# First cross attention: where the seventh pair of row maxima stands, and in which PSUM set

## The chip, the cores and the metric

The kernel runs on one NeuronCore of a Trainium2 chip. The metric is the device time of one execution in microseconds; each figure without a profile is the median of several executions. The engines that matter here are TensorE (PE in the profile; PEld is its weight load), VectorE (DVE), ScalarE (ACT), GpSimd (POOL) and the DMA queues on SyncE (SP).

## What is computed

Four transformer layers in a row on x of 8 batches x 256 tokens x 256 channels. Only the cross attention of the first layer is touched. Cut to what matters:

```python
cq = heads(ci @ cq_w, NH, CHD)            # 8 batches, 16 heads of 8 channels, 256 queries
ck, cv = jnp.split(encoder_outputs @ ckv_w, 2, axis=-1)   # 1601 keys
scores = jnp.einsum('bhqd,bhkd->bhqk', q * scale, k)
p = jax.nn.softmax(scores, axis=-1)
cctx = jnp.einsum('bhqk,bhkd->bhqd', p, v)
```

## The kernel before

`cross_attention_0` does the work in 32 **units**: 8 batches times 4 groups (`NG`) of 4 heads. A unit n has these parts, all of them put on TensorE by hand in one order.

- **Keys.** Four chunks of 400 to 402 keys (`k_chunk`, L1336 to L1338, three matmuls each), split by ScalarE (`k_high`, L1140) and VectorE (L1242) into `ks`. The matmuls write half of PSUM set 1: `K_SET = (1, 1)`.
- **Maxima.** The softmax subtracts each query's maximum over all keys. The 16 items q0 to q15 (`maxima`) each make a pair of matmuls (L1357, two row groups of the array side by side) into a set of two banks, and VectorE takes both maxima in one reduction (L1254), which adds one to `maxed`. `M_SET[q]` names the set, `m_ps[0]` or `m_ps[1]`. Items 8 to 15 and 0 to 7 give two halves; `negative_maxima` closes each half (L1262).
- **Shift.** GpSimd spreads the maxima on a diagonal, `shift` (L1365) turns them on TensorE into set 1, VectorE adds them to the queries (L1269).
- **Scores and values.** 13 key tiles (`KT`). For each, `scores` makes two matmuls (L1377), ScalarE the exponentials (L1165), `values` (L1388) adds p times v in `av_ps`.
- **Sum.** After tile 12 VectorE copies the result (L1276). A matmul (L1503, into set 1, `SUM_SET`) picks the row sums, ScalarE takes the logarithm (L1172, `ln_ready`) and its exponential with a minus sign (L1178), GpSimd multiplies.

The units overlap. `step(u, nxt)` runs t = 1 to 13 over the tiles of unit u, and the place of every other item is in tables by t. `after` is the unit behind `nxt`:

- `max_at`: maxima of `nxt` (q7 at t = 1, q8 at t = 2, up to q14 and q15 at t = 8);
- `k_at`: key chunks of `after` at t = 2, 3, 5, 6;
- `max_after_at`: maxima of `after` already (q0 at t = 9 up to q6 at t = 13).

In a step TensorE has the scores of tile t + 1, the first item of `max_at`, the key chunk, the values of tile t, then what is left. Tile 13 and 14 of a unit are tiles 0 and 1 of the next. At t = 13 the order is: scores of the next unit's tile 1, values of its tile 0, the sum (L1503), and behind the sum q6 of `after`.

The text calls a **boundary** the stretch from the sum of one unit to the first key chunk, key (0,0), at t = 2 of the next step. An item waits until the one that used its set before was read. That is given by `FREED`, the number of reductions of that unit to be done. q7 waits at `FREED[7] = 7`, for the reduction of q6. key (0,0) waits for `ln_ready`: the sum in set 1 must be read.

Batches 0 to 5 run in a loop of three turns (`units`, two batches a turn), batches 6 and 7 are written out behind it. `ahead` starts unit 0 and the first maxima of unit 1.

Of the kernel before, what the change touches and what calls it, by code (L numbers as in the profile page):

```python
# [15 lines left out]
KT = -(-NK // P)  # L16
# [370 lines left out]
PRIME = 4  # L387
# [616 lines left out]
def cross_attention_0(nc, src, c, ph, early, ahead_, out_d):  # L1004
# [4 lines left out]
    with ph:  # L1009
# [11 lines left out]
        stored, ln_ready = ph.sems2("stored"), ph.sem("ln_ready")  # L1021
# [6 lines left out]
        NM = 4 * NC  # L1028
        ROWS = (slice(0, 64), slice(64, P))

        max_at = {1: (7,), 2: (8,), 3: (9,), 4: (10,), 5: (11,), 6: (12,), 7: (13,), 8: (14, 15)}
        max_after_at = {9: (0,), 10: (1, 2), 11: (3,), 12: (4, 5), 13: (6,)}
        M_SET = (0, 1, 0, 0, 1, 0, 0, 0, 0, 0, 0, 0, 0, 0, 0, 1)
        FREED = {2: 1, 3: 3, 5: 4, 6: 6, 7: 7, 8: 8, 9: 9, 10: 10, 11: 11, 12: 12, 13: 13, 14: 14}
        M_SET_AHEAD = tuple(q % 2 for q in range(NM))
        K_SET, K_SET_AHEAD, V_SET, SHIFT_SET, SUM_SET = (1, 1), (0, 1), (0, 1), 1, 1
        k_at, v_at, shift_at = {2: (0, 0), 3: (0, 1), 5: (1, 0), 6: (1, 1)}, 4, 11
# [14 lines left out]
        with nc.Block() as block:  # L1052
# [182 lines left out]
            def _(dve):  # L1235
# [63 lines left out]
                def ahead(u):  # L1299
                    second = following(u, NG)  # L1300
                    for i in range(2):
                        for h in range(2):
                            k_half(u, i, h, K_SET_AHEAD)
                    for q in range(NM):
                        maxima(u, q, M_SET_AHEAD)
                        if q == 8:
                            negative_maxima(u, 0)
                    negative_maxima(u, 1)
                    for i in range(2):
                        for h in range(2):  # L1310
                            k_half(second, i, h, K_SET_AHEAD)
                    maxima(second, 0, M_SET_AHEAD)
                    add_shift(u)
                    for q in range(1, 7):
                        maxima(second, q, M_SET_AHEAD)

                def step(u, nxt):
# [6 lines left out]
            def _(pe):  # L1324
# [67 lines left out]
                def max_item(nxt, after, q):  # L1392

                    n = nxt[3]
                    if q == 11 and nxt[2] == 0:
                        pe.wait_ge(cv_ready, nxt[0] * 2 + 1 + PRIME)
                    elif q == 15 and after:
                        pe.wait_ge(k_ready, after[3] * 4 + 4 + PRIME)
                    elif q == 15:
                        pe.wait_ge(ln_ready, n - 1 + PRIME)  # L1400
                    else:
                        pe.wait_ge(maxed, n * NM + FREED[q] + PRIME)
                    maxima(nxt, q)
# [10 lines left out]

                def key_item(nxt, after, i, h):
                    if i == 0 and h == 0:
                        pe.wait_ge(ln_ready, nxt[3] - 1 + PRIME)
                    elif i == 1 and nxt[2] == 0 and h == 0:
                        pe.wait_ge(cv_ready, nxt[0] * 2 + 2 + PRIME)
                    elif i == 1 and nxt[2]:  # L1420
                        pe.wait_ge(k_ready, after[3] * 4 + h + 1 + PRIME)
                    k_chunk(after, i, h)
# [11 lines left out]
                def ahead(u):  # L1434
# [16 lines left out]
                    pe.wait_ge(cv_ready, 2 + PRIME)  # L1451
                    scores(tile(u, None, 0))
                    scores(tile(u, None, 1))
                    for q in range(1, 7):
                        if q == 1:
                            pe.wait_ge(shifted, 1 + PRIME)
                        else:
# [5 lines left out]
                def step(u, nxt):  # L1463
                    b, p, g, n = u
                    after = nxt and following(nxt, NG)
                    for t in range(1, KT + 1):
# [21 lines left out]
                        if nxt and nxt[2] == 0 and t == v_at:  # L1488
# [1 line left out]
                            values_made(nxt, 0)  # L1490
                            pe.wait_ge(k_ready, after[3] * 4 + 2 + PRIME)
                            values_made(nxt, 1)
                        for q in later[first:] if t < KT else ():
                            max_after_item(nxt, after, q)
                    pe.wait_ge(av_copied, n + 1 + PRIME)

# [4 lines left out]
                    else:  # L1501
                        pe.wait_ge(ln_ready, n + PRIME)
                    nc.tensor.matmul(m_ps[SUM_SET][:, 0:S], c["sum8"][:], av[:], start=True, stop=True).then_inc(sum_ready, 1)  # L1503
                    if after:
                        for q in max_after_at[KT]:
                            max_after_item(nxt, after, q)

                units(pe, NG, ahead, step)

# [1819 lines left out]
```

## Time and profile before

| what | us |
|---|---|
| median of 3 executions | 3669.23 |
| lowest and highest | 3666.94, 3672.79 |
| the profiled execution, its own time | 3663.52 |
| its span, first to last instruction | 3661.7 |
| TensorE busy, all stages | 3410.2 (93%) |
| VectorE busy | 2020.0 (55%) |
| ScalarE busy | 1840.7 (50%) |
| first cross attention | about 430 to 1255 us of the span |

The page gives busy time for the whole program, which has many stages. For one stage one reads the timeline of each engine in the same window and compares starts. A group "x2" is two instructions merged into one row. Matmuls overlap, so the distance from one start to the next is what a piece costs, and not its duration.

### The profile page before, as it was taken

Reading aid. Unit: us, or ns where it says so; the run is one execution under the profiler, and the core shown is the slowest. Engines: PE = TensorE matmul, PEld = TensorE weight load, DVE = VectorE, ACT = ScalarE, POOL = GpSimd, SP = SyncE. Lnnn points to the kernel's source line nnn. Section 1 sums busy time; section 2 is a strip of 40 time slices with the busy share of each in tenths; the row PEclk is TensorE's granted clock in tenths of the full one; section 3 lists DMA queues with packets and bytes.
Section 4 is the critical chain, followed back from the end, with each engine's and each line's share of the span. In section 5 each row is a group of like instructions: output and inputs, shape, how many; then the busy total and the mean of one; then the engine's idle time right before and its main releaser. Section 6 shows DMA issues by size and latency. Waiting matters only on the chain. (4 is left out here: it accounts for less than half of the span.)

```text
span 3661.7 us, 74076 instructions
## 1 busy us (share of the span) xinstructions
PE 3410.2 (93%) x25048; PEld 2314.4 (63%) x25048; DVE 2020.0 (55%) x3324; ACT 1840.7 (50%) x3374; POOL 1588.5 (43%) x1421
## 2 busy tenths in 40 slices
PE   7798889898999799989999999999999998999997
PEld 5555644444444388866666666666666665878886
DVE  4455577677777454435555555555555553113454
ACT  2244367666677534335555555555555553333333
POOL 3212112122211011116777777777777775004554
PEclk9899899999999899989999999999999999999998
DMA  4775200000000212230000000000001002210200
GB/s 122 166 111 116 100 7 16 18 17 18 18 16 27 96 74 99 101 117 7 16 31 13 32 13 31 13 32 13 31 14 59 13 13 103 88 68 16 97 7 12
DMA packets 74751, 179.36 MB, mean 49 GB/s; under 512 B 14720, under 2 KB 44928, under 8 KB 68480
## 3 DMA queue, kind: packets, MB, share of 16 engines
q1 hardware_dynamic: 70240, 161.81, 14.6%
q0 software_dynamic: 4128, 12.60, 1.3%
q8 instruction: 221, 3.62, 0.4%
q14 instruction: 162, 1.33, 0.1%
HBM read 115.09 MB, written 59.26 MB: 48 GB/s over the span
## 5 line engine op out<-in xcount | busy, mean ns | idle before, releaser
L1652 POOL TENSOR_TENSOR cross_acc<-cross_acc,cross_probs 128x512 f32<-128x512 f32 (+1 forms) x704 | 920.6, 1308 | 160.3 <-ACT cross_probs L1715 118.9
L1715 ACT ACTIVATE cross_probs<-cross_s,cross_bias 128x512 f32<-128x512 f32 (+1 forms) x832 | 529.6, 684 | 490.0 <-PE cross_s L1934 488.2
L1811 DVE TENSOR_REDUCE cross_partmax<-cross_r 128x1 f32<-128x400 f32 (+1 forms) x1024 | 541.8, 570 | 343.1 <-PE cross_r L1904 325.2
L1254 DVE TENSOR_REDUCE cross_partmax<-cross_m 128x2 f32<-128x800 f32 (+1 forms) x512 | 497.1, 992 | 186.4 <-PE cross_m L1357 185.4
L1165 ACT ACTIVATE cross_probs<-cross_s 128x512 f32<-128x512 f32 (+1 forms) x832 | 453.5, 595 | 151.2 <-PE cross_s L1377 150.9
L1947 PE MATMUL cross_av<-cross_probs,cross_v 128*64 128x256 f32 (+1 forms) x3328 | 458.1, 393 | 0.0
L1947 PEld LDWEIGHTS cross_av<-cross_probs,cross_v 128*64 128x64 f32 (+1 forms) x3328 | 199.2, 136 | 172.7 <-ACT cross_probs L1715 76.6
L1104 POOL TENSOR_TENSOR cross_diag<-c_ident,cross_negmax 128x256 fp32r<-128x256 f32 x128 | 75.8, 613 | 495.0 <-DVE cross_negmax L1262 495.0
L1388 PE MATMUL cross_av<-cross_probs,cross_v 128*32 128x256 f32 (+1 forms) x3328 | 268.9, 395 | 10.0 <-ACT cross_probs L1165 8.5
L1928 PE MATMUL cross_s<-cross_q_hi,cross_k_hi 64*128 64x256 f32 (+1 forms) x1664 | 253.5, 299 | 0.0
L1800 DVE TENSOR_TENSOR cross_k_lo<-cross_r,cross_k_hi 128x400 fp32r<-128x400 f32 (+1 forms) x256 | 146.5, 572 | 192.1 <-ACT cross_k_hi L1693 192.1
L1357 PE MATMUL cross_m<-cross_ks,cross_qd 64*128 64x400 f32 (+1 forms) x1024 | 211.1, 417 | 43.2 <-DVE cross_partmax L1254 35.1
L1934 PE MATMUL cross_s<-cross_shf,c_ones_r 64*128 64x256 f32 (+1 forms) x1664 | 236.5, 278 | 0.0
L1932 PE MATMUL cross_s<-cross_q_hi,cross_k_lo 64*128 64x256 f32 (+1 forms) x1664 | 236.2, 278 | 0.0
L1930 PE MATMUL cross_s<-cross_q_lo,cross_k_hi 64*128 64x256 f32 (+1 forms) x1664 | 236.0, 278 | 0.0
L1904 PE MATMUL cross_r<-cross_k_hi,cross_q_hi 64*128 64x400 f32 (+1 forms) x1024 | 212.9, 399 | 5.4 <-issue 5.3
L1377 PE MATMUL cross_s<-cross_qd,cross_ks 64*128 64x512 f32 (+1 forms) x832 | 202.8, 472 | 9.1 <-issue 8.6
L1928 PEld LDWEIGHTS cross_s<-cross_q_hi,cross_k_hi 64*128 64x128 f32 (+1 forms) x1664 | 155.0, 181 | 75.1 <-issue 71.6
L1357 PEld LDWEIGHTS cross_m<-cross_ks,cross_qd 64*128 64x128 f32 x1024 | 97.4, 190 | 153.9 <-DVE cross_partmax L1254 114.8
L2356 PE MATMUL tail_in<-tail_xe,tail_wi 128*128 128x256 f32 x768 | 173.3, 381 | 3.5 <-DVE tail_xe L2260 3.5
L1904 PEld LDWEIGHTS cross_r<-cross_k_hi,cross_q_hi 64*128 64x128 f32 x1024 | 101.5, 186 | 111.1 <-issue 83.1
L2356 PEld LDWEIGHTS tail_in<-tail_xe,tail_wi 128*128 128x128 f32 x768 | 146.9, 191 | 24.5 <-DVE tail_xe L2260 4.2
(307 smaller groups left out, 6504.2 us busy)
## 6 DMA issues: line engine op xcount, KB each, us to landing
d_masked_ctx<-tail_ctx_split SPq DMA_DIRECT2D x8, 1602.0 KB, 5.3
d_self_qk<-selfproj_qk_split POOLq DMA_DIRECT2D x32, 256.0 KB, 5.5
self_qs<-d_self_qk SPq DMA_DIRECT2D x64, 128.0 KB, 7.7
self_ks<-d_self_qk SPq DMA_DIRECT2D x64, 128.0 KB, 8.3
d_cross<-tail_pr SPq DMA_DIRECT2D x8, 1024.0 KB, 4.6
cross_qp<-d_cross SPq DMA_DIRECT2D x64, 128.0 KB, 2.2
d_cross<-cross_out SPq DMA_DIRECT2D x64, 128.0 KB, 1.8
tail_attn<-d_cross SPq DMA_DIRECT2D x8, 1024.0 KB, 5.4
```

The lines of the kernel that those rows point to most:

```text
L1165: nc.scalar.activation(probs[0:w, buf, 2 * r:2 * r + 2], s_ps[bank(of_tile, r)][0:w].rearrange("p (h s) -> p h s", h=2), ACT.Exp, scale=CH ...
L1254: nc.vector.tensor_reduce(partmax[:, :, jt // 2, jt % 2, i:i + 1], m_pair(sets[q], w), AX.X, ALU.max).then_inc(maxed, 1)
L1357: last = nc.tensor.matmul(m_ps[sets[q]][:, r * 512:r * 512 + w], qd[ROWS[r], g, j, t * P:(t + 1) * P], ks[ROWS[r], g, k0:k0 + w], start=Tr ...
L1388: last = nc.tensor.matmul(av_ps[32 * j:32 * j + 32, 0:S], v[0:w, p, t, 4 * g + j], probs[0:w, (g * KT + t) % 4, j], start=(t == 0), stop=( ...
L1652: nc.gpsimd.tensor_tensor(acc[0:w, g % 2], left, probs[0:w, slot % NPB], ALU.add).then_inc(added, 1)
L1715: nc.scalar.activation(probs[0:w, (g * KT + t) % NPB], src_, ACT.Exp, scale=XHD ** -0.5, bias=bias[0:w, p, t:t + 1]).then_inc(probs_ready, 1)
L1811: nc.vector.tensor_reduce(partmax[:, m, i:i + 1], r_ps[MAX_BANK[q]][:, 0:KCH[i][1]], AX.X, ALU.max).then_inc(maxed, 1)
L1904: nc.tensor.matmul(r_ps[MAX_BANK[q]][:, 0:w], q_hi[ROWS[h], g % 2, t * P:(t + 1) * P], k_hi[ROWS[h], g % 2, k0:k0 + w], start=True, stop=T ...
L1928: nc.tensor.matmul(o[h], k_hi[ROWS[h], x, keys], q_hi[ROWS[h], x], start=True, stop=False)
L1934: last = nc.tensor.matmul(o[h], c["ones_r"][ROWS[h], 0:w], shf[ROWS[h], x], start=False, stop=True)
L1947: last = nc.tensor.matmul(av_ps[h * XHD:(h + 1) * XHD, 0:S], v[0:w, g // 4, t, d0:d0 + XHD], probs[0:w, (g * KT + t) % NPB, h], start=(t = ...
L2356: last = nc.tensor.matmul(in_ps[n % 3][:, h * S:(h + 1) * S], wi[2 * e + h][:, k, t * P:(t + 1) * P], xe[:, b % 2, e, k], start=(k == 0), ...
```

## The change

q6 of the unit behind, which stood behind the sum at t = 13, goes to the first step of the next unit (t = 1): behind the scores of tile 2 and ahead of the values of tile 1. q7 goes behind those values, and from set 0 to set 1. The waits follow:

- q7 waits for `ln_ready` (the sum in set 1 was read) in place of the reduction of q6;
- q8 waits for seven reductions, that of q6, since q6 used set 0 before it;
- key (0,0) waits for eight reductions, that of q7, in place of `ln_ready`.

`ahead` makes q1 to q5 of unit 1 in place of q1 to q6. No matmul, reduction or activation is added or taken away. The diff:

```diff
--- before.py
+++ after.py
@@ -1028,10 +1028,10 @@
         NM = 4 * NC
         ROWS = (slice(0, 64), slice(64, P))
 
-        max_at = {1: (7,), 2: (8,), 3: (9,), 4: (10,), 5: (11,), 6: (12,), 7: (13,), 8: (14, 15)}
-        max_after_at = {9: (0,), 10: (1, 2), 11: (3,), 12: (4, 5), 13: (6,)}
-        M_SET = (0, 1, 0, 0, 1, 0, 0, 0, 0, 0, 0, 0, 0, 0, 0, 1)
-        FREED = {2: 1, 3: 3, 5: 4, 6: 6, 7: 7, 8: 8, 9: 9, 10: 10, 11: 11, 12: 12, 13: 13, 14: 14}
+        max_at = {1: (6, 7), 2: (8,), 3: (9,), 4: (10,), 5: (11,), 6: (12,), 7: (13,), 8: (14, 15)}
+        max_after_at = {9: (0,), 10: (1, 2), 11: (3,), 12: (4, 5)}
+        M_SET = (0, 1, 0, 0, 1, 0, 0, 1, 0, 0, 0, 0, 0, 0, 0, 1)
+        FREED = {2: 1, 3: 3, 5: 4, 6: 6, 7: 5, 8: 7, 9: 9, 10: 10, 11: 11, 12: 12, 13: 13, 14: 14}
         M_SET_AHEAD = tuple(q % 2 for q in range(NM))
         K_SET, K_SET_AHEAD, V_SET, SHIFT_SET, SUM_SET = (1, 1), (0, 1), (0, 1), 1, 1
         k_at, v_at, shift_at = {2: (0, 0), 3: (0, 1), 5: (1, 0), 6: (1, 1)}, 4, 11
@@ -1311,7 +1311,7 @@
                             k_half(second, i, h, K_SET_AHEAD)
                     maxima(second, 0, M_SET_AHEAD)
                     add_shift(u)
-                    for q in range(1, 7):
+                    for q in range(1, 6):
                         maxima(second, q, M_SET_AHEAD)
 
                 def step(u, nxt):
@@ -1392,7 +1392,9 @@
                 def max_item(nxt, after, q):
 
                     n = nxt[3]
-                    if q == 11 and nxt[2] == 0:
+                    if q == 7:
+                        pe.wait_ge(ln_ready, nxt[3] - 1 + PRIME)
+                    elif q == 11 and nxt[2] == 0:
                         pe.wait_ge(cv_ready, nxt[0] * 2 + 1 + PRIME)
                     elif q == 15 and after:
                         pe.wait_ge(k_ready, after[3] * 4 + 4 + PRIME)
@@ -1414,7 +1416,7 @@
 
                 def key_item(nxt, after, i, h):
                     if i == 0 and h == 0:
-                        pe.wait_ge(ln_ready, nxt[3] - 1 + PRIME)
+                        pe.wait_ge(maxed, nxt[3] * NM + 8 + PRIME)
                     elif i == 1 and nxt[2] == 0 and h == 0:
                         pe.wait_ge(cv_ready, nxt[0] * 2 + 2 + PRIME)
                     elif i == 1 and nxt[2]:
@@ -1451,7 +1453,7 @@
                     pe.wait_ge(cv_ready, 2 + PRIME)
                     scores(tile(u, None, 0))
                     scores(tile(u, None, 1))
-                    for q in range(1, 7):
+                    for q in range(1, 6):
                         if q == 1:
                             pe.wait_ge(shifted, 1 + PRIME)
                         else:
@@ -1490,7 +1492,7 @@
                             values_made(nxt, 0)
                             pe.wait_ge(k_ready, after[3] * 4 + 2 + PRIME)
                             values_made(nxt, 1)
-                        for q in later[first:] if t < KT else ():
+                        for q in later[first:]:
                             max_after_item(nxt, after, q)
                     pe.wait_ge(av_copied, n + 1 + PRIME)
 
@@ -1501,9 +1503,6 @@
                     else:
                         pe.wait_ge(ln_ready, n + PRIME)
                     nc.tensor.matmul(m_ps[SUM_SET][:, 0:S], c["sum8"][:], av[:], start=True, stop=True).then_inc(sum_ready, 1)
-                    if after:
-                        for q in max_after_at[KT]:
-                            max_after_item(nxt, after, q)
 
                 units(pe, NG, ahead, step)
```

On TensorE, at a boundary inside the loop (m0 and m1 are the two sets, s0 to s2 the banks of the scores, av0 that of the values; rows of semaphore registers are left out). Before:

```order
1363 L1503 MATMUL cross0_m1<-cross0_av,c_sum8 128x256
...
1365 L1357 MATMUL cross0_m0<-cross0_ks,cross0_qd 128x400 x2
...
1367 L1377 MATMUL cross0_s1<-cross0_qd,cross0_ks 128x512
...
1369 L1377 MATMUL cross0_s2<-cross0_qd,cross0_ks 128x512
...
1371 L1357 MATMUL cross0_m0<-cross0_ks,cross0_qd 128x402 x2
...
1373 L1388 MATMUL cross0_av0<-cross0_probs,cross0_v 32x256 x4
...
1379 L1357 MATMUL cross0_m0<-cross0_ks,cross0_qd 128x400 x2
1380 L1336 MATMUL cross0_m1<-cross0_c_hi,cross0_wk_hi 128x400
```

After:

```order
1364 L1505 MATMUL cross0_m1<-cross0_av,c_sum8 128x256
...
1366 L1377 MATMUL cross0_s1<-cross0_qd,cross0_ks 128x512
...
1368 L1377 MATMUL cross0_s2<-cross0_qd,cross0_ks 128x512
...
1370 L1357 MATMUL cross0_m0<-cross0_ks,cross0_qd 128x400 x2
...
1372 L1388 MATMUL cross0_av0<-cross0_probs,cross0_v 32x256 x4
1373 L1357 MATMUL cross0_m1<-cross0_ks,cross0_qd 128x402 x2
...
1379 L1357 MATMUL cross0_m0<-cross0_ks,cross0_qd 128x400 x2
1380 L1419 REGISTER_ALU
1381 L1336 MATMUL cross0_m1<-cross0_c_hi,cross0_wk_hi 128x400
```

The pair of 400 columns (q6) went behind both scores, the pair of 402 (q7) behind the values and into m1, and the key chunk has a wait of its own (L1419).

On VectorE, the reductions behind the copy L1276 keep their number and order. Those of q6, q7, q8 before:

```order
444 L1254 TENSOR_REDUCE cross0_partmax<-cross0_m0 128x2
445 L1251 REGISTER_ALU
446 L1254 TENSOR_REDUCE cross0_partmax<-cross0_m0 128x2
447 L1251 REGISTER_ALU
448 L1253 REGISTER_ALU
449 L1254 TENSOR_REDUCE cross0_partmax<-cross0_m0 128x2
450 L1262 TENSOR_REDUCE cross0_negmax<-cross0_partmax 128x4
```

After:

```order
445 L1254 TENSOR_REDUCE cross0_partmax<-cross0_m0 128x2
446 L1251 REGISTER_ALU
447 L1254 TENSOR_REDUCE cross0_partmax<-cross0_m1 128x2
448 L1251 REGISTER_ALU
449 L1253 REGISTER_ALU
450 L1254 TENSOR_REDUCE cross0_partmax<-cross0_m0 128x2
451 L1262 TENSOR_REDUCE cross0_negmax<-cross0_partmax 128x4
```

Only the set that the middle one reads is another.

## Rows read from the trace of the kernel before

**Rows 1.** The page, busy time: engine, us, share of the span, instructions.
```profile
PE 3410.2 (93%) x25048; PEld 2314.4 (63%) x25048; DVE 2020.0 (55%) x3324; ACT 1840.7 (50%) x3374; POOL 1588.5 (43%) x1421
```

**Rows 2.** Busy time by stretch: us, each engine's busy us, clock, DMA share, GB/s.
```profile
490.00:665.00 175.00, 160.43 (x1322) 74.02 (x1314) 134.08 (x170) 122.34 (x231) 36.41 (x51) 1.00 0.05 13
671.00:700.00 29.00, 27.23 (x199) 12.10 (x203) 21.06 (x27) 18.38 (x35) 6.29 (x9) 0.85 0.11 36
```

**Rows 3.** Line 1503, the sum: matmul passes, ns least/median/most, first and last start in us.
```profile
L1503 PE MATMUL cross_m<-cross_av,c_sum x64: 379/416/483, 490.4 to 1252.5; 128*128 128x256 f32 x64
```

**Rows 4.** Timeline of TensorE at one boundary: start, us, engine, line, tiles, count, [idle before].
```profile
817.61 0.70 PE L1503 MATMUL cross_m<-cross_av,c_sum 128*128 128x256 f32 x2 [0.17 <-DVE cross_partmax L1254]
818.51 0.45 PE L1357 MATMUL cross_m<-cross_ks,cross_qd 64*128 64x400 f32 x2 [0.20 <-DVE cross_partmax L1254]
818.80 0.41 PE L1377 MATMUL cross_s<-cross_qd,cross_ks 64*128 64x512 f32 x2
820.05 0.46 PE L1357 MATMUL cross_m<-cross_ks,cross_qd 64*128 64x402 f32 x2 [0.85 <-DVE cross_partmax L1254]
820.44 0.64 PE L1388 MATMUL cross_av<-cross_probs,cross_v 128*32 128x256 f32 x8
821.01 0.50 PE L1377 MATMUL cross_s<-cross_qd,cross_ks 64*128 64x512 f32 x2
821.60 0.45 PE L1357 MATMUL cross_m<-cross_ks,cross_qd 64*128 64x400 f32 x2
821.97 0.45 PE L1336 MATMUL cross_m<-cross_c_hi,cross_wk_hi 128*128 128x400 f32 x1
```

**Rows 5.** The same boundary, VectorE.
```profile
816.57 1.88 DVE L1254 TENSOR_REDUCE cross_partmax<-cross_m 128x2 f32<-128x800 f32 x2
819.00 0.99 DVE L1254 TENSOR_REDUCE cross_partmax<-cross_m 128x2 f32<-128x800 f32 x1 [0.55 <-PE cross_m L1357]
820.55 1.00 DVE L1254 TENSOR_REDUCE cross_partmax<-cross_m 128x2 f32<-128x804 f32 x1 [0.55 <-PE cross_m L1357]
822.17 0.99 DVE L1254 TENSOR_REDUCE cross_partmax<-cross_m 128x2 f32<-128x800 f32 x1 [0.63 <-PE cross_m L1357]
...
824.01 0.99 DVE L1254 TENSOR_REDUCE cross_partmax<-cross_m 128x2 f32<-128x800 f32 x1 [0.77 <-PE cross_m L1357]
```

**Rows 6.** The same boundary, ScalarE.
```profile
818.35 0.38 ACT L1172 ACTIVATE cross_ln_sum<-cross_m 128x256 f32<-128x256 f32 x1 [0.76 <-PE cross_m L1503]
818.63 0.59 ACT L1165 ACTIVATE cross_probs<-cross_s 128x512 f32<-128x512 f32 x1
819.10 0.42 ACT L1178 ACTIVATE cross_rsum<-cross_ln_sum 128x256 f32<-128x256 f32 x1
819.41 1.08 ACT L1165 ACTIVATE cross_probs<-cross_s 128x512 f32<-128x512 f32 x2
```

**Rows 7.** Waits of 430 to 1260 us: total, times, longest.
```profile
PEld cross_m L1357 <- DVE cross_partmax L1254: 114.8, 228, 1.3
```

**Rows 8.** Timeline of TensorE after the sum of the 31st unit.
```profile
1236.90 0.70 PE L1503 MATMUL cross_m<-cross_av,c_sum 128*128 128x256 f32 x2
1237.53 0.50 PE L1377 MATMUL cross_s<-cross_qd,cross_ks 64*128 64x512 f32 x2
1238.56 0.64 PE L1388 MATMUL cross_av<-cross_probs,cross_v 128*32 128x256 f32 x8 [0.53 <-ACT cross_probs L1165]
```

**Rows 9.** Timeline of TensorE at a boundary outside the loop.
```profile
1140.61 0.67 PE L1503 MATMUL cross_m<-cross_av,c_sum 128*128 128x256 f32 x2
...
1144.88 0.45 PE L1336 MATMUL cross_m<-cross_c_hi,cross_wk_hi 128*128 128x400 f32 x1
```

**Rows 10.** Timeline of TensorE where the loop turns.
```profile
665.38 0.45 PE L1357 MATMUL cross_m<-cross_ks,cross_qd 64*128 64x400 f32 x2 [0.20 <-DVE cross_partmax L1254]
669.73 0.91 PE L1377 MATMUL cross_s<-cross_qd,cross_ks 64*128 64x512 f32 x2 [3.90 <-issue]
...
672.96 0.70 PE L1336 MATMUL cross_m<-cross_c_hi,cross_wk_hi 128*128 128x400 f32 x1
```

## The prediction, made before the changed kernel ran

> **What bounds the kernel now.** I read the page first, then the stage. TensorE is busy 93% of the whole span [rows 1]. In 175 us of the first cross attention it is busy 160.43 us and VectorE 134.08 us [rows 2]: TensorE sets the pace, VectorE has slack, and the question is where TensorE stands still. The list of waits has one place above TensorE's others: weight loads of the maxima that wait for a VectorE reduction, 114.8 us in 228 times [rows 7]. Loads run ahead of matmuls, so that total is partly covered. The timeline shows what is not.
>
> At a boundary inside the loop [rows 4] times run from the start of the sum, 817.61, taken as 0: q6 at 0.90, scores of tile 2 at 1.19, q7 at 2.44, values of tile 1 at 2.83, scores of tile 3 at 3.40, q8 at 3.99, key (0,0) at 4.36. TensorE was idle 0.20 us before q6 and 0.85 before q7, and between scores of tile 3 and q8 lie 0.59 us, though a pair of scores lasts 0.50. All three are one chain through PSUM set 0 [rows 5]: q6's reduction starts at 819.00 and lasts 0.99, q7 starts 0.06 behind its end; q7's starts at 820.55 and lasts 1.00, q8 follows 0.05 behind its end. A turn of the chain is 1.54 us (820.05 less 818.51), of which TensorE can fill only the scores. VectorE itself waits for TensorE in each turn (0.55, 0.55, 0.63 us). So neither engine is full: the handshake over one set is the bound. There are 32 sums (64 passes, two each, 490.4 to 1252.3 us) [rows 3], and 30 of them have a q6 behind them.
>
> **The change, part by part.** I go through the new order with the rows' own distances.
>
> *Scores of tile 2 go first behind the sum.* In the 31st unit no q6 follows, and there the scores start 0.63 behind the sum (1237.53 less 1236.90) [rows 8]. Their banks are free. New: 0.63 in place of 1.19.
>
> *q6 behind these scores.* The scores last 0.50, so q6 stands at 1.13 at the latest. Its wait, q5's reduction, is over at 818.45 (816.57 + 1.88), or 0.84 [rows 5]. Its issue takes 0.29 (818.80 less 818.51), so TensorE is free at 1.42. It costs nothing, since the next piece is late anyway:
>
> *Values of tile 1* need the exponentials of tile 1. The second of them stands behind the logarithm of the sum, starts at 818.63 and lasts 0.59, to 1.61 [rows 6]. In the 31st unit, where nothing else holds them, the values start at 1.66 (1238.56 less 1236.90), after 0.53 us idle, released by ScalarE [rows 8]. New: 1.66 in place of 2.83. The cover of q6 is this wait; were it gone, q6 would cost its 0.29.
>
> *q7 behind the values, in set 1.* Values to the next piece is 0.57 (821.01 less 820.44) [rows 4], so q7 starts at 2.23. Its new wait, the logarithm, ends at 818.73, or 1.12 [rows 6]: free. Queued behind this wait on TensorE is everything, and it costs nothing as long as the logarithm is over 1.1 us early. q7's reduction starts 0.50 behind q7 (820.55 less 820.05), at 2.73; q6's was over by 1.13 + 0.49 + 0.99 = 2.61. It ends at 3.73.
>
> *Scores of tile 3, then q8.* Scores at 2.23 + 0.29 = 2.52. Exponentials of tile 2 run from 819.41, the first over by 2.34 [rows 6], so their banks are free too. q8 follows within 0.59, at 3.11 at the latest, with its wait (q6's reduction, 2.61) over, and takes 0.37 to the next piece: TensorE is free at 3.48.
>
> *key (0,0) has a new wait*, for q7's reduction: 3.73 + 0.06 = 3.79. It is met 0.3 us after TensorE is free, so it now ends the boundary. Behind it wait on TensorE the values of tile 2, and then ScalarE's and VectorE's halves of the key. New: 3.79 in place of 4.36, a gain of 0.57 us. No row shows this wait, so it has bounds. Above: values at 1.61, the end of the exponential itself, gain 0.62. Below: the 0.09 us by which the loop's boundary is longer than the one outside [rows 4, 9] once more, and 0.1 for a semaphore that comes late, gain 0.38. I take 0.57, since each link has a row of its own kind. That it could be a loss is a rival below.
>
> *Outside the loop* the same boundary takes 4.27 (1144.88 less 1140.61) [rows 9], and the new chain the same 3.79: gain 0.48.
>
> *Does the gain last?* From key (0,0) on nothing is moved. VectorE's next reduction (q9, 824.01) waited 0.77 us for TensorE [rows 5], so it shifts with it; q8's reduction, chained behind q7's, now ends near 4.65, and q9 is made later than that. No engine has a start of its own that would hold TensorE back.
>
> *Where the loop turns* (two times) TensorE waits for instructions: 3.90 us idle [rows 10]. From 669.73 (scores of tile 2) to 672.96 (key) are 3.23 us, at a lower clock: the stretch of 671 to 700 us has 0.85 [rows 2]. Now the break begins before q6, about 0.6 us earlier, but q6 (0.58 there) and the reduction of q7 (some 0.7 us) lie behind it. I put it at 0, between a gain and a loss of 0.5 each.
>
> *The start*: one maximum fewer in front, one more in step 0. 0.3 us by the same chain, between 0 and 0.6. *The last such boundary* has no key; there q9 waits for q8's reduction, and I take 0.7.
>
> **The sum.** 24 loop units less the two turns are 22 boundaries: 22 x 0.57 = 12.5. Outside, 5 x 0.48 = 2.4. Last 0.7, start 0.3, turns 0. Together 15.9 us. The profiled execution took 3663.52 and would take 3647.6; the median shown is 5.7 us above it, and 3669.2 - 15.9 gives 3653.
>
> **A rule that speaks against it.** The traced stretch with seven such boundaries, each with stops of 0.20 and 0.85 us, shows a granted clock of 1.00, that is 2.4 GHz [rows 2]. The changed boundary has stops of about 0.24 and 0.3 us. The Trainium skill, "TensorE: Matmul & The Clock Gate", section "A second HAM failure mode: psum-queue depth-cycling", says that an engine which idles briefly again and again, cycling through PSUM, can swing between its two levels. By that rule TensorE could run some of these units at 1.2 GHz; the trace of before disagrees for longer stops of the same kind.
>
> **The rivals.**
> *Eaten later (neutral).* The 0.57 us come back as a wait for ScalarE or VectorE within the next steps. For: ScalarE's exponentials release the values in the 31st unit [rows 8] and may do so in other steps. Against: VectorE's idle time is released by TensorE [rows 5], and between ScalarE's exponentials of tile 2, over by 2.9, and the key lie 0.9 us. 3664 to 3672.
> *Partly.* Slips of 0.2 to 0.4 us: a late q7, register instructions that outlast their cover, the turns. Gain 5 to 11 us: 3658 to 3664.
> *Slower: the key is held by the late q7.* The new order ties key (0,0) to ScalarE: exponential of tile 1, values, q7, reduction, key. If the values start later than 1.66 + 0.57 = 2.23, the boundary is longer than before; each 0.1 us beyond costs 3 us in 30 boundaries. At 2.6 it is 11 us: 3680. For: the ScalarE part sits behind the sum, its logarithm and a copy on VectorE. Against: 1.66 in the 31st unit, and 1.61 from ScalarE's own rows [rows 6, 8]: two readings that agree.
> *Slower: the clock swings.* TensorE falls to 1.2 GHz at the boundaries. Behind the turn, at a lower clock, scores of tile 2 to the key take 3.23 us with no wait [rows 10]; at the full clock they take 3.17, of which 0.85 is q7's wait [rows 4]. So such a boundary has 0.9 us more of TensorE's own work, and 30 of them 27, against 15.9 gained: 3680. It decides when some 18 boundaries are hit. For it speaks only the 0.85 behind the turn [rows 2], which follows a break of 3.90 us, ten times the new stops. The rule named above is the one that would give this rival.
>
> **How the numbers follow.** Forecast as summed, gain 11 to 19 us: 0.68. Partly: 0.15. Eaten: 0.09. Late q7: 0.04. Clock: 0.02. More than 19 us: 0.02. The bound of what can be told from no change is 0.2%, 7.3 us: faster than 3661.9. Of "partly" four fifths lie beyond it. Faster 0.82, same 0.12, slower 0.06. The range takes the forecast with the spread of the medians (3666.9 to 3672.8, three either side) and most of "partly": 3647 to 3661.
>
> **What would show it.** In the changed profile: scores of tile 2 at 0.6 behind the sum, values of tile 1 at 1.66, q7 at 2.23, key at 3.8, released by a VectorE reduction; some 746 us from the first to the last sum in place of 762 [rows 3]; the same distances behind the key as before. Values later than 1.8, or a key more than 0.1 behind q7's reduction, would show a step wrong; a new stop on TensorE between t = 3 and 12 would show "eaten".

## The result and the profile after

| | median us | lowest, highest | executions |
|---|---|---|---|
| before | 3668.39 | 3666.94, 3672.79 | 4 |
| after | 3638.35 | 3634.26, 3649.83 | 4 |

The first measurement gave a ratio of 0.9921, 95% interval 0.9897 to 0.9945: 30 us faster, where 16 were forecast, and under the low end of the range. The profiled execution took 3649.83 us, span 3648.1, that is 13.7 us less than the profiled one of before. Two further measurements of the same kernel, 12 executions each on two other occasions (chips 7 and 1), gave 0.9965 (0.9949 to 0.9980) and 0.9952 (0.9936 to 0.9969), medians 3644.16 and 3641.94, some 13 and 18 us faster. Every figure here leaves out one slow execution, of the kernel with the order alone (5671.55 us at a mean granted clock of 0.751). So there are two questions: is the mechanism the forecast one, and where did the first 30 us come from?

The page of the kernel after, busy time (answers to [rows 1]), and TensorE's row for the sum, now line 1505: ns least, median, most, then first and last start (answers to [rows 3]):

```profile
PE 3398.7 (93%) x25048; PEld 2313.2 (63%) x25048; DVE 2016.5 (55%) x3324; ACT 1843.3 (51%) x3374; POOL 1590.2 (44%) x1421
...
L1505 PE MATMUL cross_m<-cross_av,c_sum x64: 379/416/483, 498.8 to 1243.6; 128*128 128x256 f32 x64
```

From the first to the last pass are 744.8 us, against 762.1 before: 17.3 less, where the forecast had some 746 in place of 762. That this near hit has compensating parts in it is shown further down. The weight loads of the maxima wait less for VectorE (answer to [rows 7]):

```profile
PEld cross_m L1357 <- DVE cross_partmax L1254: 53.0, 142, 1.9
```

Timeline of TensorE at one boundary inside the loop, the kernel after (answers to [rows 4]; start, us, engine, line, operation, count, idle before and its releaser):

```profile
793.96 0.70 PE L1505 MATMUL cross_m<-cross_av,c_sum 128*128 128x256 f32 x2
794.59 0.50 PE L1377 MATMUL cross_s<-cross_qd,cross_ks 64*128 64x512 f32 x2
794.93 0.38 PE L1357 MATMUL cross_m<-cross_ks,cross_qd 64*128 64x400 f32 x2
795.62 0.64 PE L1388 MATMUL cross_av<-cross_probs,cross_v 128*32 128x256 f32 x8 [0.32 <-ACT cross_probs L1165]
796.19 0.45 PE L1357 MATMUL cross_m<-cross_ks,cross_qd 64*128 64x402 f32 x2
796.48 0.43 PE L1377 MATMUL cross_s<-cross_qd,cross_ks 64*128 64x512 f32 x2
796.71 0.38 PE L1357 MATMUL cross_m<-cross_ks,cross_qd 64*128 64x400 f32 x2
797.74 0.45 PE L1336 MATMUL cross_m<-cross_c_hi,cross_wk_hi 128*128 128x400 f32 x1 [0.65 <-DVE cross_partmax L1254]
```

Read from the sum as 0: scores of tile 2 at 0.63, q6 at 0.97, values of tile 1 at 1.66, released by ScalarE, q7 at 2.23, scores of tile 3 at 2.52, q8 at 2.75, key (0,0) at 3.78, released by VectorE. Forecast: 0.63, 1.13 at the latest, 1.66, 2.23, 2.52, 3.11 at the latest, 3.79.

VectorE at the same place (answers to [rows 5]):

```profile
795.35 0.99 DVE L1254 TENSOR_REDUCE cross_partmax<-cross_m 128x2 f32<-128x800 f32 x1 [0.55 <-PE cross_m L1357]
796.68 1.89 DVE L1254 TENSOR_REDUCE cross_partmax<-cross_m 128x2 f32<-128x804 f32 x2 [0.34 <-PE cross_m L1357]
798.49 0.16 DVE L1262 TENSOR_REDUCE cross_negmax<-cross_partmax 128x4 f32<-128x16 f32 x1
799.77 0.99 DVE L1254 TENSOR_REDUCE cross_partmax<-cross_m 128x2 f32<-128x800 f32 x1 [1.12 <-PE cross_m L1357]
```

The reductions of q7 and q8 are now one row of two, back to back. Before, each of them stood 0.55 to 0.63 us behind a wait of its own. The next one (q9) waits 1.12 us for TensorE, so VectorE does not hold the steps behind.

At 9 of the 22 boundaries inside the loop the key stands 0.09 to 0.11 us later, at 3.86 to 3.88. One of them, where the sum starts at 521.96, VectorE and then the key:

```profile
524.68 1.89 DVE L1254 TENSOR_REDUCE cross_partmax<-cross_m 128x2 f32<-128x804 f32 x2 [0.35 <-PE cross_m L1357]
...
525.82 0.44 PE L1336 MATMUL cross_m<-cross_c_hi,cross_wk_hi 128*128 128x400 f32 x1 [0.73 <-DVE cross_partmax L1254]
```

q7's reduction starts 2.72 behind the sum as at the other boundaries and lasts 0.99 to 1.00, but the key follows 0.14 behind its end in place of 0.06. That is the prediction's sign of a wrong step, "a key more than 0.1 behind q7's reduction". Why it happens at the same places of each turn was not found out.

ScalarE (answers to [rows 6]) is where it was, 0.74, 1.02 and 1.49 behind the sum:

```profile
794.70 0.38 ACT L1172 ACTIVATE cross_ln_sum<-cross_m 128x256 f32<-128x256 f32 x1 [0.76 <-PE cross_m L1505]
794.98 0.59 ACT L1165 ACTIVATE cross_probs<-cross_s 128x512 f32<-128x512 f32 x1
795.45 0.42 ACT L1178 ACTIVATE cross_rsum<-cross_ln_sum 128x256 f32<-128x256 f32 x1
```

What the stage does not explain lies ahead of it. The first sum stands at 498.8 us in this execution, against 490.4 before, although no instruction ahead of the stage was changed. The stretch of 10 to 430 us, before and then after (us, busy us of each engine, clock, DMA share, GB/s), holds the same 2248 matmuls:

```profile
10.00:430.00 420.00, 348.93 (x2248) 249.26 (x2248) 218.53 (x414) 141.01 (x278) 92.93 (x98) 0.92 0.58 127
```
```profile
10.00:430.00 420.00, 353.75 (x2248) 251.44 (x2248) 218.02 (x413) 139.46 (x276) 93.05 (x98) 0.91 0.57 125
```

The same matmuls took 4.8 us more of TensorE at a lower granted clock. The kernel before, run again, has its first sum at 500.3 us, so this belongs to the execution and not to the change. A single execution can lose or win as much as half of what this change is worth.

### The profile page after: what moved, and what is told of

It is laid out like the page before. It is cut to its first block and busy times, and to the rows that moved or that the text cites. A ratio compares the mean times of both kernels' runs of the same rounds, so it can differ in the third digit from the quotient of the medians.

```text
span 3648.1 us, 74076 instructions
## 1 busy us (share of the span) xinstructions
PE 3398.7 (93%) x25048; PEld 2313.2 (63%) x25048; DVE 2016.5 (55%) x3324; ACT 1843.3 (51%) x3374; POOL 1590.2 (44%) x1421
## 3 DMA queue, kind: packets, MB, share of 16 engines
q8 instruction: 221, 3.62, 0.4%
```

## The experiments

Twelve runs on three chips (7, 13 and 1), each against 19 to 29 executions of the kernel before on its own chip. "Mean clock" is TensorE's granted clock, the mean over a run's executions (of the profiled one alone in the two rows of first profiles). "Key" is the start of key (0,0) behind the sum at a boundary inside the loop, "stage" the time from the first to the last sum of the profiled execution, in us. The stage is read from one execution, to the first pass of the last sum; the last pass, used above, starts 0.4 later.

| kernel | key | stage | ratio to before | 95% interval | mean clock |
|---|---|---|---|---|---|
| before (first profile) | 4.36 | 761.7 | | | 0.968 |
| after (first profile) | 3.78 | 744.5 | | | 0.967 |
| before again | 4.36 | 758.6 | 1.0007 | 0.9993, 1.0021 | 0.970 |
| after again | 3.77 | 741.9 | 0.9965 | 0.9949, 0.9980 | 0.970 |
| after, third time | 3.77 | 744.7 | 0.9952 | 0.9936, 0.9969 | 0.971 |
| new order alone | 4.36 | 773.8 | 1.0038 | 1.0019, 1.0056 | 0.966 |
| new order alone, again | 4.36 | 772.6 | 1.0028 | 1.0009, 1.0046 | 0.966 |
| new set alone | 3.33 | 731.9 | 0.9934 | 0.9914, 0.9954 | 0.970 |
| after, ScalarE 0.3 later | 4.08 | 753.6 | 0.9986 | 0.9966, 1.0006 | 0.968 |
| before, ScalarE 0.3 later | 4.36 | 757.2 | 1.0012 | 0.9997, 1.0028 | 0.970 |
| after, exponential first | 3.39 | 732.3 | 0.9917 | 0.9885, 0.9950 | 0.971 |
| new set, exponential first | 3.34 | 731.4 | 0.9933 | 0.9908, 0.9958 | 0.969 |
| new set, key behind values | 3.63 | 724.9 | 0.9921 | 0.9891, 0.9951 | 0.968 |
| the same again | 3.62 | 724.7 | 0.9917 | 0.9897, 0.9937 | 0.969 |

### Each kernel once more

No edit. What was expected of the kernel before:

> The kernel before once more, nothing changed. It tells how far two profiles and two medians of the same kernel lie apart. Theory A (the first cross attention gained 17 us, what lies beyond it in the medians is TensorE's low-clock stretches falling elsewhere in other stages): ratio to the kernel before 1.000 within 0.2%, but single executions and the stages outside differ by up to 10 us with the mean clock. Theory B (the change moves other stages too): the executions agree within 3 us and the stages outside the first cross attention take the same time in each profile of this kernel.

Measured: ratio 1.0007, and single executions from 3651.45 us (clock 0.973) to 3673.74 (clock 0.968). The first cross attention took 758.6 against 761.7 in the first profile. Theory A holds in that executions of one kernel differ by 20 us. The median of these 12, 3664.37, is 7 us above that of the 29 others of the same kernel on the same chip, 3657.26.

> The changed kernel once more. Theory A: from the first to the last sum again 744.5 us within 1.5, and the median 14 to 20 us under the kernel before, since the 30 us of the first measurement were 17 from the change and the rest from clock stretches of those executions. Theory B: again some 30 us under, with stages outside the first cross attention shorter by a fixed amount of 10 us or more.

Measured: 0.9965 and a stage of 741.9 us, 16.7 under the kernel before run again. The median of 3644.16 is 13 us under that of before. Both are just outside what theory A named (14 to 20 us, and a stage of 744.5 within 1.5), and far from theory B's 30.

> The changed kernel a third time. Theory A (the change is worth what the stage shows, 16 to 17 us; the first medians differed by more since few executions were compared and each one's mean clock moves it by up to 15 us): first to last sum 742 to 745 us, ratio to before 0.9955, 0.994 to 0.998. Theory B (something else is gained outside the stage): ratio at or under 0.993.

Measured: 0.9952, stage 744.7. Theory A. In both repeats the interval excludes the 0.993 of theory B, and the first measurement's 0.9921 as well.

The executions show what separates them. The 89 of the kernel before that stand in these runs reach from 3643.15 us at a mean granted clock of 0.976 (chip 7) to 3679.78 at 0.966 (chip 13). The 41 on chip 7 alone reach from 3643.15 to 3673.74. A line through all 192 executions of all kernels, one slope and a level for each kernel, has 2.6 us for 0.001 of mean clock and leaves 3.1 us unexplained. The text calls the difference between two levels of this line the difference **at equal clock**. For the changed kernel it is 15.8 us under before, give or take 1.5. Two things limit it. It is a relation over these runs, not an experiment with a single cause changed. And where a kernel itself brings more low clock, as the next one does, this figure leaves that loss out.

The first four executions of the changed kernel fit this. Three of them ran at a mean clock of 0.973 or 0.974, where the 24 later ones have 0.9706 on average. The later ones at 0.973 or 0.974 took 3633.58 to 3644.85 us, and the three took 3634.26 to 3638.67.

### The order alone

The changed kernel with q7 back in set 0 and the waits of before:

```diff
-        M_SET = (0, 1, 0, 0, 1, 0, 0, 1, 0, 0, 0, 0, 0, 0, 0, 1)
-        FREED = {2: 1, 3: 3, 5: 4, 6: 6, 7: 5, 8: 7, 9: 9, 10: 10, 11: 11, 12: 12, 13: 13, 14: 14}
+        M_SET = (0, 1, 0, 0, 1, 0, 0, 0, 0, 0, 0, 0, 0, 0, 0, 1)
+        FREED = {2: 1, 3: 3, 5: 4, 6: 6, 7: 7, 8: 8, 9: 9, 10: 10, 11: 11, 12: 12, 13: 13, 14: 14}
...
-                    if q == 7:
-                        pe.wait_ge(ln_ready, nxt[3] - 1 + PRIME)
-                    elif q == 11 and nxt[2] == 0:
+                    if q == 11 and nxt[2] == 0:
...
-                        pe.wait_ge(maxed, nxt[3] * NM + 8 + PRIME)
+                        pe.wait_ge(ln_ready, nxt[3] - 1 + PRIME)
```

> The changed kernel with the seventh pair back in set 0: q7 waits for q6's reduction, q8 for q7's, key (0,0) for the logarithm, as before; only the order on TensorE is the new one. Theory (the set is what gains): q7 at 2.50, q7's reduction over at 4.0, q8 at 4.05, key at 4.42 behind the sum against 4.36 before: no gain, 0 to 3 us slower than before. Rival (the order gains, by putting work beside the wait): key near 3.8, 15 us faster.

Timeline of TensorE at a boundary of this kernel:

```profile
809.08 0.70 PE L1503 MATMUL cross_m<-cross_av,c_sum 128*128 128x256 f32 x2 [0.17 <-DVE cross_partmax L1254]
809.70 0.50 PE L1377 MATMUL cross_s<-cross_qd,cross_ks 64*128 64x512 f32 x2
810.05 0.38 PE L1357 MATMUL cross_m<-cross_ks,cross_qd 64*128 64x400 f32 x2
810.74 0.64 PE L1388 MATMUL cross_av<-cross_probs,cross_v 128*32 128x256 f32 x8 [0.31 <-ACT cross_probs L1165]
811.52 0.45 PE L1357 MATMUL cross_m<-cross_ks,cross_qd 64*128 64x402 f32 x2
811.81 0.40 PE L1377 MATMUL cross_s<-cross_qd,cross_ks 64*128 64x512 f32 x2
813.07 0.45 PE L1357 MATMUL cross_m<-cross_ks,cross_qd 64*128 64x400 f32 x2 [0.85 <-DVE cross_partmax L1254]
813.44 0.45 PE L1336 MATMUL cross_m<-cross_c_hi,cross_wk_hi 128*128 128x400 f32 x1
```

The wait of 0.85 us did not go. It moved from q7 to q8, and the key stands at 4.36 (813.44 less 809.08) as before, where 4.42 was expected. The order by itself gains nothing: the set gains. What was not expected (0 to 3 us) is that it is 0.28% to 0.38% slower, 10 to 14 us, with the same key. So it ran once more:

> The new order with q7 in set 0 once more. The first time its key stood at 4.36 as before and yet it was 0.38% slower, at a lower mean clock (0.966 against 0.970). Theory (its longer stops bring TensorE to its lower level more often): mean clock again under 0.968 and the time 5 to 15 us over before. Rival (chance of the executions): clock 0.970 and the time within 4 us of before.

Measured again: 1.0028, mean clock 0.966. The theory holds against chance. At equal clock the two runs are 1.5 us over before, give or take 1.6: nearly all of the loss goes with the lower clock. The stage in both profiled executions has a lower clock than before, here the kernel before and then the two of the order alone, over the stage:

```profile
430.00:1255.00 825.00, 745.85 (x5968) 343.31 (x5968) 606.78 (x768) 556.76 (x1050) 150.67 (x216) 0.97 0.06 17
```
```profile
430.00:1280.00 850.00, 756.28 (x5972) 350.37 (x5971) 608.34 (x770) 559.64 (x1051) 150.65 (x216) 0.95 0.06 17
```
```profile
430.00:1280.00 850.00, 755.90 (x5972) 350.22 (x5972) 607.66 (x769) 559.52 (x1051) 150.77 (x216) 0.95 0.06 17
```

TensorE's busy time grew by 10 us for the same matmuls. One of the falls, behind a boundary:

```profile
736.42 0.45 PE L1357 MATMUL cross_m<-cross_ks,cross_qd 64*128 64x400 f32 x2 [0.86 <-DVE cross_partmax L1254]
736.80 0.53 PE L1336 MATMUL cross_m<-cross_c_hi,cross_wk_hi 128*128 128x400 f32 x1
...
737.92 1.08 PE L1388 MATMUL cross_av<-cross_probs,cross_v 128*32 128x256 f32 x8
```

The values take 1.08 us in place of 0.64. Here the prediction's clock rival is seen at work, in a kernel whose stops at a boundary are 0.31, some 0.2 and 0.85 us, a little more than the 0.20 and 0.85 of before. At the plain boundaries of the changed kernel, whose stops are 0.32 and 0.65, none of its three profiles has such a fall. Behind the rows: the Trainium skill, "TensorE: Matmul & The Clock Gate", section "A second HAM failure mode: psum-queue depth-cycling", says that an engine with many brief stops can swing between its levels. These rows agree for the order alone and not for the plain boundaries of the changed kernel. What exactly decides stays open.

Two places of the changed kernel do lose by the clock. The first is the start of the stage, 32 us from the first scores, before and then after:

```profile
458.00:490.00 32.00, 27.90 (x199) 12.57 (x200) 23.22 (x30) 17.58 (x33) 2.37 (x4) 0.79 0.00 1
```
```profile
465.00:497.00 32.00, 27.74 (x186) 12.54 (x186) 22.03 (x28) 16.71 (x31) 2.37 (x4) 0.74 0.00 1
```

In the same time it gets 186 matmuls done and not 199. From the first scores to the first sum are 31.4 and 31.6 us in the two profiles of before, 31.3 with the set alone, 32.8 to 32.9 in the three of the changed kernel, and 33.3 and 33.4 in the two of the order alone: the new order costs 1.3 us there or more. The second place is the second turn of the loop, 28 us of before and then of after:

```profile
864.00:892.00 28.00, 23.59 (x184) 10.35 (x184) 19.40 (x25) 17.43 (x33) 3.09 (x5) 0.94 0.12 39
```
```profile
860.00:888.00 28.00, 23.87 (x168) 10.74 (x166) 17.08 (x22) 15.96 (x30) 3.10 (x5) 0.82 0.12 39
```

The third profile of the changed kernel has 0.82 here too, the second 0.94 as before. The other way round, the kernel before falls once at a plain boundary outside the loop, in both of its profiles, and the changed one in none:

```profile
1193.00:1205.00 12.00, 11.32 (x77) 5.16 (x77) 7.24 (x10) 7.78 (x15) 1.91 (x3) 0.86 0.06 15
```

### The set alone

The kernel before with q7 in set 1 and its waits, q6 left behind the sum:

```diff
-        M_SET = (0, 1, 0, 0, 1, 0, 0, 0, 0, 0, 0, 0, 0, 0, 0, 1)
-        FREED = {2: 1, 3: 3, 5: 4, 6: 6, 7: 7, 8: 8, 9: 9, 10: 10, 11: 11, 12: 12, 13: 13, 14: 14}
+        M_SET = (0, 1, 0, 0, 1, 0, 0, 1, 0, 0, 0, 0, 0, 0, 0, 1)
+        FREED = {2: 1, 3: 3, 5: 4, 6: 6, 7: 5, 8: 7, 9: 9, 10: 10, 11: 11, 12: 12, 13: 13, 14: 14}
...
-                    if q == 11 and nxt[2] == 0:
+                    if q == 7:
+                        pe.wait_ge(ln_ready, nxt[3] - 1 + PRIME)
+                    elif q == 11 and nxt[2] == 0:
...
-                        pe.wait_ge(ln_ready, nxt[3] - 1 + PRIME)
+                        pe.wait_ge(maxed, nxt[3] * NM + 8 + PRIME)
...
-                            pe.wait_ge(maxed, NM + q - 1 + PRIME)
+                            pe.wait_ge(maxed, NM + q - 1 + (q == 6) + PRIME)
```

> The kernel before with the seventh pair in set 1 and its three waits, q6 left behind the sum as before (the sixth pair of the start waits for the fifth's reduction). Theory (the set is what gains, and the new order costs, since it puts q7 behind values that wait for ScalarE): q6 at 0.90, q7 at 1.5, its reduction over at 3.3, key at 3.4 against 4.36 before and 3.77 after: 22 x 0.96 + 5 x 0.9 = 26 us under before, 9 to 11 under the changed kernel. Rival (both parts are needed): key at 3.8 or later, no better than the changed kernel.

```profile
787.33 0.70 PE L1505 MATMUL cross_m<-cross_av,c_sum 128*128 128x256 f32 x2 [0.16 <-DVE cross_partmax L1254]
788.22 0.45 PE L1357 MATMUL cross_m<-cross_ks,cross_qd 64*128 64x400 f32 x2 [0.20 <-DVE cross_partmax L1254]
788.51 0.42 PE L1377 MATMUL cross_s<-cross_qd,cross_ks 64*128 64x512 f32 x2
788.74 0.37 PE L1357 MATMUL cross_m<-cross_ks,cross_qd 64*128 64x402 f32 x2
789.04 0.64 PE L1388 MATMUL cross_av<-cross_probs,cross_v 128*32 128x256 f32 x8
...
790.66 0.45 PE L1336 MATMUL cross_m<-cross_c_hi,cross_wk_hi 128*128 128x400 f32 x1 [0.21 <-DVE cross_partmax L1254]
```

The key is at 3.33 (790.66 less 787.33), the stage 731.9 us, 30 under the first profile of before and 12.6 under after. The ratio of 0.9934 is 24 us under before. At equal clock it is 26, and 10 under after (give or take 3). The ratios' intervals just touch, 0.9914 to 0.9954 and 0.9949 to 0.9980 on this chip, but key and stage say the same. So half of the change, the other set, is worth more than the whole. The new order costs some 10 us of it, since it puts q7 behind values that wait for ScalarE; the exponential first, below, takes this wait away, and the stage is then as short as here.

### ScalarE later

One more ScalarE instruction behind each unit's logarithm, first in the kernel after, then in that of before (`spare` is a buffer that nobody reads, `spare_ready` its semaphore):

```diff
                     nc.scalar.activation(ln_sum[:], m_ps[SUM_SET][:, 0:S], ACT.Ln).then_inc(ln_ready, 1)
+                    act.wait_ge(spare_ready, n + PRIME)
+                    nc.scalar.activation(spare[:].rearrange("p (t s) -> p t s", t=2),
+                        c["ident"][:].unsqueeze(1).to_broadcast([P, 2, P]), ACT.Copy).then_inc(spare_ready, 1)
```

> The changed kernel with one more ScalarE instruction behind the logarithm of each unit, a copy of a constant 128x256 into a buffer that nobody reads. It puts the second exponential of tile 1 later by its own start-to-start time, some 0.28 us. Theory (key (0,0) hangs on the chain exponential, values, q7, reduction): values of tile 1 at 1.94 behind the sum, q7 at 2.51, key at 4.05; 30 boundaries x 0.28 = 8 us slower than the changed kernel, so 7 us under before. Rival (VectorE or TensorE has another reason for 3.77): key stays at 3.8 and the time with it.

The kernel after with it, values of tile 1 and then the key:

```profile
795.52 0.70 PE L1508 MATMUL cross_m<-cross_av,c_sum 128*128 128x256 f32 x2 [0.17 <-DVE cross_partmax L1257]
...
797.48 0.64 PE L1391 MATMUL cross_av<-cross_probs,cross_v 128*32 128x256 f32 x8 [0.62 <-ACT cross_probs L1166]
...
799.60 0.45 PE L1339 MATMUL cross_m<-cross_c_hi,cross_wk_hi 128*128 128x400 f32 x1 [0.65 <-DVE cross_partmax L1257]
```

The values went from 1.66 to 1.96, the key from 3.78 to 4.08: every 0.1 us of ScalarE arrives at the key in full. In the time it is 9 us at equal clock (expected 8). That is the price law of the rival "key held by the late q7".

> The kernel before with the same spare ScalarE instruction behind the logarithm, 0.28 us in each unit. Theory: before the change the boundary hung on the chain through set 0, and the values of tile 1 stood behind q7 at 2.82 with the exponential long over: key stays at 4.36, time within 2 us of before. Rival (the instruction itself costs, wherever it stands, so that the 9 us of the changed kernel with it prove nothing): 6 us or more slower.

In the kernel before the key stayed at 4.36 and the stage at 757.2 us. The ratio of 1.0012 (0.9997 to 1.0028) is 4 us and allows from none to 10, so by itself it does not rule out the rival, 6 us or more. At equal clock it is 2.5 us, give or take 1.9, against 9 in the changed kernel, and that does. The stage agrees: it is the shortest of the three profiles with a key at 4.36 and both pairs in the order of before. The instruction costs where the chain goes through ScalarE, and not for itself.

### The exponential first

ScalarE makes the second exponential of tile 1 ahead of the logarithm:

```diff
-                    if before and t == 1:
-                        log_sum(before)
...
                     if now:
                         exponentials(now, 1)
                     if before and t == 1:
+                        log_sum(before)
                         inverse_sum(before)
```

> The changed kernel with ScalarE's logarithm moved behind the second exponential of tile 1, which no longer waits for the sum. Theory: values of tile 1 follow q6 on TensorE at 1.3 to 1.4, q7 at 1.9, its reduction chained to q6's from 2.4 to 3.4, key at 3.45 against 3.77: 29 x 0.32 = 9 us under the changed kernel. Rival: the logarithm now comes later or another wait takes over, key at 3.77 or later.

```profile
788.49 0.70 PE L1504 MATMUL cross_m<-cross_av,c_sum 128*128 128x256 f32 x2 [0.17 <-DVE cross_partmax L1253]
...
789.76 0.64 PE L1387 MATMUL cross_av<-cross_probs,cross_v 128*32 128x256 f32 x8
...
791.88 0.45 PE L1335 MATMUL cross_m<-cross_c_hi,cross_wk_hi 128*128 128x400 f32 x1 [0.51 <-DVE cross_partmax L1253]
```

Measured on top of the changed kernel: values of tile 1 at 1.27, with no wait, q7 at 1.84, key at 3.39, stage 732.3, ratio 0.9917. At equal clock 13 us under after, where 9 were expected; the stage is 10 to 12 us shorter. The theory holds.

> Both: the seventh pair in set 1 with the order of before, and the logarithm behind the exponential. Theory: there q7 stands ahead of the values, and the key hangs on the two chained reductions of q6 and q7, not on ScalarE: key at 3.35 as without the second edit, time within 2 us of the seventh pair in set 1 alone. Rival (ScalarE holds TensorE there too): 5 us or more faster than that.

On top of the set alone: key at 3.34 and stage 731.4 against 3.33 and 731.9; ratio 0.9933 against 0.9934. The theory holds there too: with q7 ahead of the values ScalarE is off the path, and what is left is the pair of reductions of q6 and q7.

### The key behind the values

On top of the set alone, key (0,0) behind the values of tile 2:

```diff
-                        if after and t in k_at:
+                        if after and t in k_at and t > 2:
                             key_item(nxt, after, *k_at[t])
...
                         if now:
                             values(now)
+                        if after and t == 2:
+                            key_item(nxt, after, *k_at[t])
```

> The seventh pair in set 1 with the order of before, and key (0,0) behind the values of tile 2 in place of ahead of them, so that the values fill the wait for q7's reduction. Theory: values of tile 2 at 3.0 (released by ScalarE at 2.94), key at 3.55 with no wait, scores of tile 4 at 4.3 against 4.65: 29 x 0.35 = 10 us under the seventh pair in set 1 alone, some 35 under before. Rival: the later key makes ScalarE's and VectorE's halves late, and a new stop at t = 3 to 5 takes it back.

```profile
780.77 0.70 PE L1507 MATMUL cross_m<-cross_av,c_sum 128*128 128x256 f32 x2
...
783.83 0.64 PE L1388 MATMUL cross_av<-cross_probs,cross_v 128*32 128x256 f32 x8
784.40 0.45 PE L1336 MATMUL cross_m<-cross_c_hi,cross_wk_hi 128*128 128x400 f32 x1
```

Values at 3.06, key at 3.63 with no wait, scores of tile 4 at 4.37 in place of 4.65. The stage is 724.9 us, 7 under the set alone; 10 were expected.

> q7 in set 1 with the order of before and key (0,0) behind the values of tile 2, once more, beside the changed kernel. Theory: first to last sum 725 us against 743, so 15 to 20 us under the changed kernel and 32 to 37 under before. Rival: its stage is shorter but the low-clock stretches take it back, within 8 us of the changed kernel.

Measured: 0.9917 again, stage 724.7, median 3631.28, 31 us under before. In plain medians that is 11 us under the changed kernel on the same chip, less than the 15 to 20 expected; its mean clock is 0.969 against 0.971. At equal clock it is 33 under before and 17 under after. It beats both kernels. Against the exponential first on the changed kernel (0.9917, 6 executions) the runs do not decide.

## Why the prediction was right in its main steps and wrong in its range

- **What bounds the kernel now:** right. The chain through set 0 was the bound. The order alone left it and gained nothing, the set alone broke it and gained 24 us.
- **Part by part:** right within 0.02 us at each piece that binds: scores 0.63, values 1.66, q7 2.23, key 3.78 against 3.79. At 9 of the 22 boundaries the key stands at 3.86 to 3.88. The prediction's lower bound allowed for that by "0.1 for a semaphore that comes late", a figure that no row gave; the runs have 0.09 to 0.11 there.
- **Does the gain last:** right. From sum to sum 23.75 became 23.17 at many boundaries inside the loop and 23.31 became 22.79 outside. In the first pair of profiles the 22 boundaries gained between 0.46 and 0.67, 0.57 on average without a fall of the clock, as forecast, and those outside 0.52 against 0.48. The distance from key to the next sum did not grow, the turns left out. "Eaten later" is out.
- **The last boundary:** 20.94 to 20.16, 0.78 against 0.7.
- **The turns of the loop, put at 0:** mis-sized. The distances from sum to sum there are 29.35 and 27.66 in the first profile of before and 27.47 and 27.64 in the second, against 28.40 and 29.90, 28.34 and 27.13, 28.46 and 29.88 in the three of after. On average that is 56.1 us before and 57.4 after for the two together, a loss of 1.3, each profile moved by falls of the clock of up to 2 us.
- **The start, put at a gain of 0.3:** wrong in sign. It is a loss of 1.3 us, in all three profiles, with a lower clock. Neither term allowed for a longer stretch at the lower level of the clock.
- **The rule on the clock:** the prediction set against it that the trace of before shows 1.00 in seven boundaries. It missed that the same trace falls at a boundary far from any turn, at 1193 to 1205 us, a stretch with a granted clock of 0.86.
- **The sum:** 15.9 us forecast. In the first pair of profiles the stage gained 17.2: 12.5 from the 22 boundaries, 2.6 from the five outside and 0.8 from the last, which make 15.9. To these come 2.6 from two falls of the clock that only the profile of before has, and 1.3 go at the turns. The start's loss lies ahead of the first sum. From the first scores to the last sum the means are 791.7 us before (two profiles) and 776.6 after (three), 15.1 less. So the chain was forecast exactly, and that the total came near too is in part luck: losses at the start and the turns against falls of the clock in before. The two later ratios give 13 and 18 us.
- **The step that failed is the spread of the medians, "three either side".** It was read off the three executions of before, which happened to lie within 6 us. The same kernel reaches from 3643 to 3680 us in 89 executions. The median of before was high for it (3668.4, against 3661 over these 89) and that of the first four executions after was low (3638.4 against 3643 over the later 24). 7 and 5 us in opposite directions make 12 of the 14 us that were missing, and the rest is within the intervals. For after, the clock of the first executions shows why the median was low. For before it stays open: of its first four executions neither the clocks nor the chip are on record. A term that was wanted in the range is the difference of two medians of three or four executions, and it is nearly as large as the gain.
- **The rivals:** the late q7 is a true mechanism, shown by the spare instruction, with the price that was named; it did not come since ScalarE was on time. The clock rival did not strike the plain boundaries of the changed kernel, cost it 1.3 us at the start and about as much at the turns, and struck the order alone for 8 to 13 us in the medians. Its chance of 0.02 was low for a mechanism that putting one pair back into the other set, with its waits, brings about.

## What to carry to other kernels

When a chain over one buffer bounds an engine, ask first which single entry breaks it, and cost the rest of the edit apart: here the other PSUM set alone was worth 26 us at equal clock, and with the new order around it 16. Place the piece that others wait for ahead of work that waits for a third engine. And before a gain under 0.5% is measured or forecast, take the spread from many executions with their mean clock, not from three medians.

## What the runs showed of the hardware

- Executions of one kernel differ by 0.8% on one chip (3643 to 3674 us in 41) and by 1.0% over three (3643 to 3680 in 89), and the mean granted clock of TensorE goes along: 2.6 us for each 0.001.
- A chain TensorE, VectorE, TensorE over one PSUM set costs 0.49 to 0.50 us from the start of a pair of matmuls to the reduction, the reduction's 0.99 to 1.00, and 0.05 to 0.06 to the next piece: 1.54 us in the kernel before (818.51 to 820.05), 1.55 with the order alone (811.52 to 813.07) and in the changed one (796.19 to 797.74). At 9 of 22 boundaries of the changed kernel the last part is 0.14.
- The same work with a somewhat longer sum of brief stops (0.31, 0.2 and 0.85 us at a boundary, in place of 0.20 and 0.85) ran the stage at a granted clock of 0.95 in place of 0.97, in both its profiles. Which property of the stops does it was not found out: the changed kernel with ScalarE later has 0.62 and 0.65, a longer sum than the kernel before, and a mean clock of 0.968.
